# Self attention: a batch's values loaded ahead of queries and keys, and the second half of the maxima between the two score blocks

## The reference, cut to what matters

```python
q, k = apply_rotary(q, k, position_ids, l)
# sdpa, causal:
scores = jnp.einsum('bhqd,bhkd->bhqk', q * scale, k)
scores = jnp.where(jnp.tril(ones), scores, finfo.min)
p = jax.nn.softmax(scores.astype(jnp.float32), axis=-1)
ctx = jnp.einsum('bhqk,bhkd->bhqd', p, v)
```

## Time and profile before

| what | before |
|---|---|
| median of 3 runs | 3669.23 us (3666.94 to 3672.79) |
| profiled execution | 3663.52 us |
| its span | 3661.7 us |
| TensorE matmul busy | 3410.2 us, 93% of the span |
| VectorE, ScalarE, GpSimd busy | 2020.0, 1840.7 and 1588.5 us |
| mean granted TensorE clock | 0.968 |

### The profile page before, as it was taken

How to read it: one execution, slowest core, us unless ns; L and a number is a source line. 1 busy time by engine, 2 the same in 40 slices (tenths; PEclk the granted TensorE clock), 3 DMA queues, 4 the chain that set the end, 5 groups by cost and what they waited for, 6 DMA issues and landing times. The chain is left out here.

```text
span 3661.7 us, 74076 instructions
## 1 busy us (share of the span) xinstructions
PE 3410.2 (93%) x25048; PEld 2314.4 (63%) x25048; DVE 2020.0 (55%) x3324; ACT 1840.7 (50%) x3374; POOL 1588.5 (43%) x1421
## 2 busy tenths in 40 slices
PE   7798889898999799989999999999999998999997
PEld 5555644444444388866666666666666665878886
DVE  4455577677777454435555555555555553113454
ACT  2244367666677534335555555555555553333333
POOL 3212112122211011116777777777777775004554
PEclk9899899999999899989999999999999999999998
DMA  4775200000000212230000000000001002210200
GB/s 122 166 111 116 100 7 16 18 17 18 18 16 27 96 74 99 101 117 7 16 31 13 32 13 31 13 32 13 31 14 59 13 13 103 88 68 16 97 7 12
DMA packets 74751, 179.36 MB, mean 49 GB/s; under 512 B 14720, under 2 KB 44928, under 8 KB 68480
## 3 DMA queue, kind: packets, MB, share of 16 engines
q1 hardware_dynamic: 70240, 161.81, 14.6%
q0 software_dynamic: 4128, 12.60, 1.3%
HBM read 115.09 MB, written 59.26 MB: 48 GB/s over the span
## 5 line engine op out<-in xcount | busy, mean ns | idle before, releaser
L1652 POOL TENSOR_TENSOR cross_acc<-cross_acc,cross_probs 128x512 f32<-128x512 f32 (+1 forms) x704 | 920.6, 1308 | 160.3 <-ACT cross_probs L1715 118.9
L1715 ACT ACTIVATE cross_probs<-cross_s,cross_bias 128x512 f32<-128x512 f32 (+1 forms) x832 | 529.6, 684 | 490.0 <-PE cross_s L1934 488.2
L1811 DVE TENSOR_REDUCE cross_partmax<-cross_r 128x1 f32<-128x400 f32 (+1 forms) x1024 | 541.8, 570 | 343.1 <-PE cross_r L1904 325.2
L1254 DVE TENSOR_REDUCE cross_partmax<-cross_m 128x2 f32<-128x800 f32 (+1 forms) x512 | 497.1, 992 | 186.4 <-PE cross_m L1357 185.4
L1165 ACT ACTIVATE cross_probs<-cross_s 128x512 f32<-128x512 f32 (+1 forms) x832 | 453.5, 595 | 151.2 <-PE cross_s L1377 150.9
L1947 PE MATMUL cross_av<-cross_probs,cross_v 128*64 128x256 f32 (+1 forms) x3328 | 458.1, 393 | 0.0
L1947 PEld LDWEIGHTS cross_av<-cross_probs,cross_v 128*64 128x64 f32 (+1 forms) x3328 | 199.2, 136 | 172.7 <-ACT cross_probs L1715 76.6
L1104 POOL TENSOR_TENSOR cross_diag<-c_ident,cross_negmax 128x256 fp32r<-128x256 f32 x128 | 75.8, 613 | 495.0 <-DVE cross_negmax L1262 495.0
L1388 PE MATMUL cross_av<-cross_probs,cross_v 128*32 128x256 f32 (+1 forms) x3328 | 268.9, 395 | 10.0 <-ACT cross_probs L1165 8.5
L1928 PE MATMUL cross_s<-cross_q_hi,cross_k_hi 64*128 64x256 f32 (+1 forms) x1664 | 253.5, 299 | 0.0
L1800 DVE TENSOR_TENSOR cross_k_lo<-cross_r,cross_k_hi 128x400 fp32r<-128x400 f32 (+1 forms) x256 | 146.5, 572 | 192.1 <-ACT cross_k_hi L1693 192.1
(11 more groups left out here) (307 smaller groups left out, 6504.2 us busy)
## 6 DMA issues: line engine op xcount, KB each, us to landing
d_masked_ctx<-tail_ctx_split SPq DMA_DIRECT2D x8, 1602.0 KB, 5.3
d_self_qk<-selfproj_qk_split POOLq DMA_DIRECT2D x32, 256.0 KB, 5.5
self_qs<-d_self_qk SPq DMA_DIRECT2D x64, 128.0 KB, 7.7
self_ks<-d_self_qk SPq DMA_DIRECT2D x64, 128.0 KB, 8.3
d_cross<-tail_pr SPq DMA_DIRECT2D x8, 1024.0 KB, 4.6
cross_qp<-d_cross SPq DMA_DIRECT2D x64, 128.0 KB, 2.2
d_cross<-cross_out SPq DMA_DIRECT2D x64, 128.0 KB, 1.8
tail_attn<-d_cross SPq DMA_DIRECT2D x8, 1024.0 KB, 5.4
```

Source lines behind the costliest of these rows:

```text
L1254: nc.vector.tensor_reduce(partmax[:, :, jt // 2, jt % 2, i:i + 1], m_pair(sets[q], w), AX.X, ALU.max).then_inc(maxed, 1)
L1652: nc.gpsimd.tensor_tensor(acc[0:w, g % 2], left, probs[0:w, slot % NPB], ALU.add).then_inc(added, 1)
L1715: nc.scalar.activation(probs[0:w, (g * KT + t) % NPB], src_, ACT.Exp, scale=XHD ** -0.5, bias=bias[0:w, p, t:t + 1]).then_inc(probs_ready, 1)
L1811: nc.vector.tensor_reduce(partmax[:, m, i:i + 1], r_ps[MAX_BANK[q]][:, 0:KCH[i][1]], AX.X, ALU.max).then_inc(maxed, 1)
```

## The change

Two orders are changed, and no instruction is added or taken away. On SyncE, the values of batch b + 2 are issued in front of the queries and keys of batch b + 3, and now have a `wait_stored` of their own. On TensorE, the second half of the maxima moves from before the two score blocks to between them.

```diff
                     if g == NG - 1:
+                        if b + 2 < B:
+                            sp.wait_ge(av_ready, (b + 1) * NG + PRIME)
+                            early.wait_stored(sp, b + 2)
+                            early.values(sp, b + 2)
                         if b + 3 < B:
                             sp.wait_ge(s1_ready, (b + 1) * NG + PRIME)
                             early.wait_stored(sp, b + 3)
                             early.heads(sp, b + 3, slice(0, NP), q_loaded[b % 3])
-                        if b + 2 < B:
-                            sp.wait_ge(av_ready, (b + 1) * NG + PRIME)
-                            early.values(sp, b + 2)
...
                     values(u, 0)
                     values(u, 1)
+                    if nxt:
+                        scores(nxt, 0)
                     if after:
                         maxima(after, 1)
                     if nxt:
-                        scores(nxt, 0)
                         scores(nxt, 1)
                     sums(u)
```

## The result

| | before | after |
|---|---|---|
| median, first comparison | 3668.39 us (3666.94 to 3672.79, 4 runs) | 3633.38 us (3627.57 to 3637.97, 4 runs) |
| ratio | | 0.9902, 95% interval 0.9883 to 0.9920 |
| profiled execution, its span | 3663.52, 3661.7 us | 3630.37, 3628.6 us |
| mean, all later executions | 3661.2 us (97, standard deviation 7.6) | 3639.3 us (30, standard deviation 7.4) |
| difference of these means | | 22.0 us, 95% interval 18.9 to 25.0 |

The forecast was 3647.0 us from 3669.2, a gain of 22.2 us. The later executions are those of four more sessions, on three chips, and they give a gain of 22.0 us. With the first comparison counted in (101 and 34 executions) it is 23.0 us, 20.1 to 25.9.

What follows compares the result with a forecast made beforehand. TensorE, with gaps, was taken to bound self attention; 8.6 (maxima order) + 7.8 (waits for values) + 5.8 (clock drop) = 22.2 us, so 3669.2 would become 3647.0. The range was 3637 to 3659; the forecast had 70%.

Steps and rivals of the forecast that it cites:

- TensorE the bound, with gaps: Self attention: TensorE bounds it, busy 44.8 of 50 us, with gaps waiting for `negmax` (10.0 us) and values (7.8 us).
- Part 1: SyncE's loads: values of batch b+2 issued first land within 16.7 us, so all four TensorE waits go, 7.8 us.
- Its clock drop: Self attention: the 1.2 GHz stretch behind the 2.67 us wait for values goes with that wait, 5.8 us.
- Part 2: TensorE's order: second maxima between the score blocks no longer wait for VectorE's reductions, 24 x 0.36 = 8.6 us.
- the new seams: TensorE's new neighbours (values to scores, scores to maxima, maxima to scores): taken as 0, bounds 3 us less or more.
- The circle: Second maxima, reductions, `diag`, next unit's scores 0 and second maxima: 4.52 us, under the unit's 4.92, so no bound.
- A: Rival, 12%: seams or lock add 0.75 us to the new circle, units stay at 5.27 us; gain 13.6, time 3655.6.
- The bound that put the product's 0.73 us onto `diag`: GpSimd's product for `out` beside VectorE's `diag`: delaying `diag` would exceed the slack by 0.33, 10 us over 30 units; taken 0.
- B: Rival, 10%: DMA transfers become the bound, GpSimd waits for late stores of `out`; gain 14 to 18, time 3653.
- C: Rival, 4%: queries and keys land past 25.8 us, TensorE stands and loses its clock; 3671.6, or 3688 with all five batches.
- D: Rival, 4%: values sent first share engines with later loads, land near 17 us; only the maxima order's 8.6 us, time 3661.
- The sum: Whole kernel: 8.6 + 7.8 + 5.8 = 22.2 us gained, 0.6%, from 3669.2 to 3647.0.

Runs made afterwards that it cites:

- twelve minima: Changed kernel plus twelve spare small minima on VectorE per unit, ahead of the one that completes the maxima: 3658.35 us, ratio 0.9983 to the kernel before.

## Why the prediction was right or wrong

- **TensorE the bound, with gaps:** right. They are gone and it is busy 50.00 of 50 us.
- **Part 1, four waits of 7.8 us:** right. 13.5 us alone, where 7.8 + 5.8 less 1.8 make 11.8. The landing was taken at some 4 us and was 3.7 to 8.5; both are far under the 16.7 that the sum rests on.
- **Its clock drop, 5.8 us:** right in kind and, over many executions, about in size. Where a drop falls isn't fixed: one of four waits had one in the first profile of before, and two of five in the second. Each execution has its mean granted clock on record, and as the clock has two levels, the time at 1.2 GHz is twice the missing share of the span. It is 218.2 us on average in the 97 executions of before and 204.5 in the 30 of the changed kernel, 13.7 less (6.0 to 21.4). Among executions of one kernel, a microsecond more at 1.2 GHz goes with 0.34 us more of time. So 4.7 of the 22.0 us are clock, and 17.3 (15.9 to 18.7) are left at an equal clock, where parts 1 and 2 without the drop were worked out at 16.4. These are estimates from clocks rounded to 0.001, and they take in the clock of all stages.
- **Part 2, 0.36 us in 24 units:** right; a unit takes 4.91 us, and the new seams cost nothing. New is that this part alone is worth nothing that can be measured, as the waits for values and the time at 1.2 GHz grow.
- **The circle:** right to 0.01 us once it was made the bound. `diag` ended 0.43 us ahead of scores 0 where 0.46 was worked out. GpSimd's product did start where `diag` ends, and `diag` kept its 1.23 us; A did not occur. The bound that put the product's 0.73 us onto `diag` had the wrong engine paying, at least when `diag` starts first: with twelve minima they overlapped by 0.93 us and the product took the delay.
- **B:** GpSimd's waits for stores came, 13.4 us in three, the transfers' share rose to 0.98 in the first batch, and the cover sufficed. Nothing of it reached TensorE. C and D did not occur.
- **The sum, 22.2 us:** the stage gave 22.8 us between the first two profiles; the four later sessions give 22.0 (18.9 to 25.0). That it agrees to 0.2 us is in part luck: the interval is 6 us wide, and from profile to profile of one kernel this stage differs by 3.5 us before and by 4.9 after the change.

What failed is the last step, "what is timed is such runs: 3669.2 - 22.2 = 3647.0", and with it the range. It took the three runs shown, 5.9 us apart, as the spread of the kernel. Their median is 8.0 us above the mean of the 97 later executions, which go from 3647.0 to 3679.4. So the forecast of 3647.0 lies 7.7 us above 3639.3, where 30 executions put the changed kernel, and its four first ones fell 5.9 us below that. In the first comparison the median of before is 7.1 us above its later mean, and that of the changed kernel 5.9 us below: together the 13 us. I had bounds of 0 and 23 us for the clock behind four waits of one stage, and none for the other stages.

The lower end of the range doesn't follow from its own words either: two drops of 5.8 us and 3 us of seams below 3647.0 make 3632.4 and not 3637. The measured 3633.4 would have been inside, but by luck, since neither of these is what made the time short.

The Trainium skill (TensorE: Matmul & The Clock Gate, Part 1) states that the clock gate runs free of the kernel, which I had used for the drops of one stage only. Nothing in that is tied to one stage, and the profiles agree: in the second cross attention 28.3 to 40.6 us for the same work.

Drawing four from the 97 and four from the 30 again and again gives differences of medians from 9 to 35 us in 95 of 100 draws, and 35 or more in 2 of 100. Compared by their means the first four and four are 36.1 us apart, and only some 3 of 1000 draws reach that. So the first comparison is a rare draw, though a possible one. The clock on record for its four executions of the changed kernel, 0.971 to 0.976, accounts for some 3 of the 6 us by which their mean is below the later one; for those of before none is on record. Both executions whose profiles I first compared can be placed: 9.6 of their 33.1 us lie in one stretch at 1.2 GHz. For the other runs of that comparison no trace exists. That chance alone made the excess is the best account, not a shown one, and its cause stays open. Three chips agree on some 22 us; that the chip of the first comparison differs from them isn't excluded.

## What to carry to other kernels

Lengthen or shorten a stage by what its own trace shows, and judge the time by many executions: here medians of four were off by 6 and 7 us in opposite directions, more than half of the effect together. When a reordering removes a wait, look for the load that the wait was covering: the order of TensorE alone was worth nothing, because the values came no sooner, and it paid only behind the earlier load. When an order makes a new circle through two engines, sum it: the sum gave the unit's length to 0.01 us.

## What the runs showed of the hardware

- TensorE was busy 29.15 of 30 us and stayed at a granted clock of 0.53 in one execution; in another of the same kernel the same work had 0.88. The busy time of the rows didn't tell which level was granted.
- The length of an idle did not tell whether the clock would fall. In one execution of the kernel before, 1.2 GHz followed on an idle of 2.67 us and not on those of 0.74, 2.03 and 2.40 us; in another it followed on idles of 1.46 and 2.12 us and not on one of 2.05. Behind 3.15, 3.69, 4.34 and 4.43 us, all of one execution, it fell each time.
- Over 97 executions of the kernel before, each on one core, the times had a standard deviation of 7.6 us, and time at 1.2 GHz went with them at 0.34 us for each microsecond.
- GpSimd's product of two SBUF tiles stood while VectorE's `diag`, which reads two as well and had started first, was under way: 0.91 and 1.52 us in place of 0.73, with `diag` at its 1.23 us.
- Small operations on VectorE overlap: four of 157 ns in 0.39 us, twelve in 0.98 us, some 0.075 us each beyond the first.
